# Cross-attention and a ternary-weight FFN on one core: weight group 0 with a scale of its own, partition-first inputs, a block order per phase, gate and up product signalled apart

## What is computed

```python
def xattn(h, ctx, Wq, Wk, Wv, Wo, gq, gk):        # 16 batches, 128 queries, 128 keys, 16 heads of 128
    q = rmsnorm((h @ Wq).reshape(B, Sq, H, D), gq)    # h: (16, 128, 256), Wq: (256, 2048)
    k = rmsnorm((ctx @ Wk).reshape(B, Skv, H, D), gk) # ctx: (16, 128, 128), Wk: (128, 2048)
    v = (ctx @ Wv).reshape(B, Skv, H, D)
    attn = softmax(einsum('bqhd,bkhd->bhqk', q, k) / sqrt(D))
    return einsum('bhqk,bkhd->bqhd', attn, v).reshape(B, Sq, H * D) @ Wo
def ffn(x, w_gate, w_up, w_down, ln_weight):      # bit_linear: x rounded to 8 bits per row, w to -1, 0, 1
    h = silu(bit_linear(x, w_gate)) * bit_linear(x, w_up)     # 256 -> 1024
    return bit_linear(rms_norm(h, ln_weight), w_down)         # 1024 -> 256
x = x + xattn(layernorm(x), ctx, ...)
x = x + ffn(layernorm(x), ...)
```

## Time and profile before

| | us |
|---|---|
| median of 3 runs | 482.82 |
| the three runs | 482.82, 481.75, 487.97 |
| the profiled execution, its own time | 481.36 |
| its span in the trace | 479.6 |

### The profile page before, as it was taken

The page is one execution under the profiler, slowest core; times in us unless marked ns, Lnnn a source line. Parts: engine busy times, 40 slices in busy tenths (PEclk is TensorE's granted clock), DMA queues, the critical chain, the costliest instruction groups (busy, mean ns, idle before and its releaser), DMA issues.

```text
span 479.6 us, 14503 instructions
## 1 busy us (share of the span) xinstructions
PE 408.6 (85%) x4459; PEld 308.8 (64%) x4459; DVE 431.3 (90%) x1237; ACT 434.9 (91%) x1459; POOL 393.2 (82%) x362
## 2 busy tenths in 40 slices
PE   0228776899999999999999999999999678789985
PEld 0127555687777877878777777777787455455564
DVE  0787899899999999999999999999998857999995
ACT  2298899999999999999999999999999579999983
POOL 1007568799999999999999999999998956878882
PEclk9986998899999999999999999999999899999999
DMA  7980464356554544545545455455564441011001
GB/s 261 355 258 12 128 192 88 66 112 130 111 114 88 121 98 96 122 88 110 109 88 122 97 103 115 88 111 110 97 116 100 93 84 25 0 34 33 22 33 57
DMA packets 145326, 50.18 MB, mean 105 GB/s; under 512 B 135952, under 2 KB 143120, under 8 KB 144784
## 3 DMA queue, kind: packets, MB, share of 16 engines
q1 hardware_dynamic: 144192, 46.68, 43.9%
q10 hardware_dynamic: 1104, 3.15, 1.9%
HBM read 14.16 MB, written 2.10 MB: 34 GB/s over the span
## 4 chain that ended last, share of the span: by engine, by line
ACT 50%; issue 16%; POOL 12%; DVE 8%; PE 8%; DMA 4%; ACTq 0%; POOLq 0%; SPq 0%; DVEq 0%
ACT work L655 15%; ACT kjunk L685 8%; ACT qhl L588 6%; ACT qshl L671 5%; POOL rkq L533 4%; DMA stage<-in_wq 3%; ACT work L673 3%; ACT ohl L692 3%; POOL work L525 2%; POOL phl L541 2%; PE KQ L375 2%; PE SO L375 2%; ACT stage L647 1%; POOL stage L554 1%; POOL qshl L516 1%
## 5 line engine op out<-in xcount | busy, mean ns | idle before, releaser
L375 PE MATMUL KQ<-hT,wqs 128*128 (+1 forms) x1536 | 102.7, 225 | 20.8 <-DVE qhl L912 16.2
L655 ACT ACTIVATE work<-SO,nbias,rkq 128x128 f32<-128x128 f32 x256 | 115.6, 483 | 3.1 <-DVE nbias L930 2.8
L533 POOL TENSOR_TENSOR rkq<-kqe,negh 128x8 f32<-128x8 f32 x65 | 111.8, 1721 | 5.0 <-DVE kqe L920 3.9
L375 PEld LDWEIGHTS KQ<-hT,wqs 128*128 128x128 f16 x1536 | 94.9, 101 | 28.1 <-issue 17.6
L516 POOL TENSOR_TENSOR qshl<-work,qshl 128x512 f16<-128x512 f32 x64 | 74.3, 1161 | 31.5 <-ACT work L673 31.4
L375 PE MATMUL EB<-As,ohl 128*128 128x256 f16 x768 | 96.4, 276 | 0.0
L375 PEld LDWEIGHTS EB<-As,ohl 128*128 128x128 f16 x768 | 76.2, 99 | 23.4 <-issue 0.8
L541 POOL TENSOR_TENSOR phl<-work,phl 128x512 f16<-128x512 f32 x64 | 74.1, 1158 | 7.2 <-DVE phl L970 5.4
L525 POOL TENSOR_TENSOR work<-work,rinv 128x512 f32<-128x512 f32 x64 | 66.6, 1041 | 4.3 <-DVE rinv L890 4.2
L375 PEld LDWEIGHTS SO<-kT,qhl 128*128 128x128 f16 x768 | 44.1, 98 | 31.4 <-DMA kT<-khl 20.3
L375 PE MATMUL SO<-kT,qhl 128*128 128x128 f16 x768 | 53.7, 219 | 7.1 <-ACT work L655 3.4
(11 more groups left out here) (153 smaller groups left out, 911.6 us busy)
## 6 DMA issues: line engine op xcount, KB each, us to landing
xs<-in_x SPq DMA_DIRECT2D x4, 512.0 KB, 8.8
wvo<-in_wo SPq DMA_DIRECT2D x1, 2048.0 KB, 24.6
out<-wqs SPq DMA_DIRECT2D x16, 128.0 KB, 1.7
raw<-in_ctxT ACTq DMA_DIRECT2D x1, 1024.0 KB, 5.8
stage<-in_wk SPq DMA_DIRECT2D x1, 1024.0 KB, 13.5
stage<-in_wq SPq DMA_DIRECT2D x1, 1024.0 KB, 16.5
stage<-in_wq ACTq DMA_DIRECT2D x1, 1024.0 KB, 12.8
kT<-khl SPq DMA_TRANSPOSE x64, 2.9
```

The lines of the kernel that those rows point to most:

```text
L375: last = matmul(out, lhsT=left(i), rhs=right(j), start=start and n == 0, stop=stop and n == 2)
L533: pool.tensor_tensor(rkq[:, g % 4, :], kqe[:, g % 2, :], negh[:, 0:2 * HG], ALU.pow).then_inc(root_ok, 1)
L655: ins = act.activation(pe[:, s, c], SB[:, c], ACT.Exp, scale=rkq[:, (g - AT_X + 1) % 4, HG + h:HG + h + 1], bias=nbias[:, s, h:h + 1], acc ...
```

## The change

The change has these parts.

1. **Inputs laid out partition first.** x, context, Wq (by group), Wv, Wo and the FFN weights are arranged on the host so that each partition's row is one contiguous piece (4 to 16 KB where 512 B to 4 KB were).
2. **Loads in SP's queue**, in the order x of batches 0 to 3, Wk of group 0, Wq of group 0, the rest of Wk, Wq of groups 1 to 3, Wv, Wo, context, the rest of x. ACT's queue keeps the transposed context and gq, gk.
3. **Group 0 has its own factors.** The first reduction takes the maximum over Wq group 0 and the sum over Wk group 0 only; a second reduction (`second_maxima` on PE, `maxima(2, ...)` on DVE) makes `scl[:, 4:6]` for groups 1 to 3. ACT's high splits of those wait for it.
4. **Squares of Wv and Wo** in ACT's queue at steps 0 (two) and 1 (one); the total and the factor of A (`TOT_AT`) at step 2, where it was step 1.
5. **An order per phase.** `step` is cut into named parts, called by `fill` (steps 0 to 3), `early` (4 to 7), `step` (the loop) and `drain` (after it).
6. **Gate and up split.** The gate product waits for the silu of the block before and signals silu by itself (`f_g`); the up product waits for h of the block before; silu writes two buffers in turn.

```diff
-SQ_AT = {0: (0, 1), 1: (1, 3)}
-STAT_AT = {0: (1, 3), 3: (3, 4)}
+SQ_AT = {0: (0, 2), 1: (2, 3)}
+STAT_AT = {0: (1, 3), 1: (3, 4)}
...
-        HI_AT = {'start': (0, 5), 0: (5, 9), 3: (9, 10), 4: (10, 11), 5: (11, 12)}
+        HI_AT = {'start': (0, 3), 0: (3, 8), 2: (8, 11), 3: (11, 12)}
...
             x_load(0)
-            sp.dma_start(wk_f, wk).then_inc(wk_in, 16)
-            sp.dma_start(wq_f[:, 1, :], wq[P:2 * P]).then_inc(wq_in[1], 16)
+            sp.dma_start(wk_f[:, 0:GW], wk[:, 0:GW]).then_inc(wk_in[0], 16)
+            sp.dma_start(wq_f[:, 0, :, :], wqP[:, 0, :, :]).then_inc(wq_in[0], 16)
+            sp.dma_start(wk_f[:, GW:INNER], wk[:, GW:INNER]).then_inc(wk_in[1], 16)
+            for g in range(1, G):
+                sp.dma_start(wq_f[:, g, :, :], wqP[:, g, :, :]).then_inc(wq_in[g], 16)
...
+            def second_maxima(b, g):
+                if now(b, g) == 0:
+                    te.wait_ge(amax2_ok, 1)
+                    te.wait_ge(asum_ok, 3)
+                    te.transpose(MB[0:2, P:2 * P], amax2[:, :], ident_f[:, :]).then_inc(gT_ps, 1)
+                    te.wait_ge(gdiag_ok, 2)
+                    te.matmul(MB[:, 8:10], lhsT=ones_f[0:2, :], rhs=gdiag[0:2, 0:2], start=True,
+                              stop=True).then_inc(gmax_ps, 1)
...
+                    need(te, f_sil, b, g, AT_GU, 1)
+                    ffn_product(KQ, wgq, s).then_inc(f_g, 1)
+                if live(b, g, AT_GU, B):
+                    s = (g - AT_GU) % 2
+                    need(te, f_xT, b, g, AT_GU)
                     need(te, f_hh, b, g, AT_GU, 1)
...
+                    ffn_product(TM, wuq, s).then_inc(f_gu, 1)
```

More of the change, by code:

```diff
@@ L323, in straight, with steps @@
                 step(s // G, s % G)
-        def steps(eng, step, ffn):
-            straight(step, 0, 2 * G)
+        def steps(eng, fill, early, step, drain, ffn):
+            straight(fill, 0, G)
+            straight(early, G, 2 * G)
             with eng.Fori(2, 2 + F_CHUNKS) as b:
@@ L542, in step, with fill, early, drain @@
                                        ALU.subtract).then_inc(plo_ok, 1)
+            def fill(b, g):
+                A_root(b, g)
+                roots_at(b, g)
+                q_square_low(b, g)
+                kq_roots(b, g)
+                c_lows(b, g)
+            def early(b, g):
+                q_square_low(b, g)
+                c_lows(b, g)
+                p_scaled(b, g)
+                kq_roots(b, g)
+                roots_at(b, g)
+                A_root(b, g)
+                p_low(b, g)
+            def step(b, g):
+                q_square_low(b, g)
+                p_scaled(b, g)
+                kq_roots(b, g)
+                p_low(b, g)
+            def drain(b, g):
+                ffn_roots_first(b, g)
+                q_square_low(b, g)
+                p_scaled(b, g)
+                kq_roots(b, g)
+                p_low(b, g)
             def ffn(b, g):
@@ L574, in ffn @@
                                        ALU.mult).then_inc(f_cg, 1)
-            steps(pool, step, ffn)
+            steps(pool, fill, early, step, drain, ffn)
         @block.scalar
@@ L736, in ffn @@
                     act.wait_ge(f_nm, 2)
-            steps(act, step, ffn)
+            steps(act, fill, early, step, drain, ffn)
         @block.vector
@@ L1172, in step, with fill, early, drain @@
                     ins.then_inc(e_ps, 1)
+            def fill(b, g):
+                scores(b, g)
+                second_maxima(b, g)
+                q_product(b, g)
+                k_product(b, g)
+                q_sums(b, g)
+                A_total(b, g)
+                A_products(b, g)
+                ln_transposed(b, g)
+            def early(b, g):
+                q_product(b, g)
+                k_product(b, g)
+                q_sums(b, g)
+                scores(b, g)
+                e_product(b, g)
+                A_products(b, g)
+                output(b, g)
+                A_total(b, g)
+                ln_transposed(b, g)
+                second_maxima(b, g)
+                ffn_sums(b, g)
+            def step(b, g):
+                q_product(b, g)
+                q_sums(b, g)
+                k_product(b, g)
+                scores(b, g)
+                output(b, g)
+                e_product(b, g)
+            def drain(b, g):
+                q_product(b, g)
+                q_sums(b, g)
+                k_product(b, g)
+                scores(b, g)
+                output(b, g)
+                e_product(b, g)
+            def ffn_product(banks, w, s):
+                for i in range(2):
+                    for k in range(KT):
+                        ins = te.matmul(banks[:, i * 512:(i + 1) * 512], lhsT=fxT[:, s, k, :],
+                                        rhs=w[:, k, i * 512:(i + 1) * 512], start=k == 0, stop=k == KT - 1)
+                return ins
             def ffn(b, g):
@@ L1219, in ffn @@
                     ins.then_inc(f_y, 1)
-            steps(te, step, ffn)
+            steps(te, fill, early, step, drain, ffn)
 _OUT = (B, SQ, DM)
```

339 lines of the change are left out of this document (259 added, 80 removed).

## The result

The changed kernel takes 480.42 us (median of 20 runs, 477.98 to 486.29), the kernel before 485.25 (20 runs beside them, 479.55 to 490.06). The ratio is 0.9924, 95% interval 0.9901 to 0.9947: 3.7 us faster (2.6 to 4.8), about half of the 7.0 that was forecast. The profiled execution took 482.9 us, its span is 481.1.

A forecast was written before the change was run, and what follows sets the result against it. ACT was taken to bound the start and, with other engines, a full loop; DVE's and ACT's work the FFN. Gains of 5.0 (start) and 2.0 (FFN) off 481.36 gave 474.4, 474.5 as median; range 470.5 to 480.0.

The forecast's parts named there:

- Nothing is to be had in it: Main loop: engines full and same instructions in the same order, so its length stays at 278.3 us.
- The first factors: Start, on DVE: ready at 13.8 instead of 23.08, 9.3 us earlier, needing only group 0 of Wk and Wq.
- near range: Start: the loads needed for the first factors land between 9.4, when gk is in, and 10.1.
- The ledger of ACT, 56.3 us and 1.0 idle: Steps 0 to 7: from q pieces at 28.4, ACT's work plus idle time puts the loop's start at 85.7.
- The start's gain, 5.0 us: Start and steps 0 to 7: the loop's first exponentials come at 85.7 against 90.71.
- The FFN, 2.0 us: FFN: splitting gate from up breaks a 4.5 us ring; blocks fall no lower than 4.4; bounds 0 and 3.85.
- The 0.5 for block 1: FFN: the part of its 2.0 us gained ahead, where block 1 waits for its silu.
- From the profile to the median: Whole kernel: 474.4 for a profiled execution became 474.5 for the changed kernel's median.
- early steps idle as before: Rival, steps 0 to 7: ACT's 4.26 us of waits stay and the FFN gives 1.0; 478.8 us, chance 0.16.
- The late first group: Rival, start: x of four batches lands at 11.18, Wk and Wq of group 0 at 13.1; 477.5 us, chance 0.09.
- the FFN weights ahead of the transposes: Rival, early steps: kT and pT wait behind 3 MB in SP's queue, delaying scores; 486.5 us, chance 0.05.
- the Trainium skill's rule on small transfers: Start: batch transfers to 1 MiB or more; by it the first loads land about 13.6, 3.5 us more.

The follow-up runs named there:

- before_freed: Kernel before with khl, kT, phl and pT at multiples of 512 bytes and kT's transpose ahead of pT's at every step; 479.23 us, ratio 0.986.
- loads_only: Kernel before with only the changed kernel's transfers, layouts and queues; block orders, factors and FFN as before; 483.77 us, ratio 0.995.
- gk_first: Changed kernel with gq and gk issued ahead of the transposed context on ACT's queue; 484.26 us, ratio 0.995.
- small_tiles_last: Changed kernel with its two new small tiles allocated behind all others, so khl, kT, phl and pT keep their old addresses; 478.00 us, ratio 0.986.
- aligned_512: Changed kernel with two unused tiles that put khl, kT, phl and pT each at a multiple of 512 bytes; 476.77 us, ratio 0.985.
- before_again: Kernel before, nothing edited, profiled a second time; 485.23 us.
- khl_off_64: Kernel before with unused tiles that move only khl, the transposes' source, 64 bytes beyond a multiple of 256; 487.83 us.

## Why the prediction was wrong

The forecast was 474.5; it was 480.4. Without the 2.9 us of the first point it would have been 477.5. By its own steps:

- **"Nothing is to be had in it", the loop of unchanged length.** The step that failed. "The same instructions in the same order" was true, and I took the same length from it. The transposes of k in it, whose order and bytes were the same, landed in 3.1 us for 2.9, and with p's transpose ahead of them in the queue that wait was on the path of the scores. Twelve iterations of 20.38 for 20.14 are 2.9 us lost, by two small tiles that moved khl by 64 bytes. Shown in both directions, and on the one side of the transposes. In the other direction the kernel had 6.7 us to gain by the same transposes (before_freed).
- **The first factors.** 14.88 for 13.8. The near range, 9.4 to 10.1 for the landings, had the right rows, but gk, which landed after 7.7 us in the earlier trace rows, took 9.4, with the same context ahead of it on ACT's queue and other transfers on SP's, and the maximum started at 11.34. In loads_only it took 10.7. It was one of three things due there: in gk_first the next, Wq's group 0, let it start at 10.7 and no earlier, and ACT's sums came last. Over six traces the q pieces come 4.1 us earlier (29.21 for 33.31 over seven), not 4.7.
- **The ledger of ACT, 56.3 us and 1.0 idle.** The work was right. The idle time was 2.56 us: 0.71 where I had 0.6, and 1.85 in step 3, where ACT waits for two products of Wv and Wo. PE did them near half its clock, in 1.93 and 1.91 us, where the pair of the step before took 1.11 and 1.03. Windows of PE (busy, clock, DMA share, GB/s), the changed kernel:

```profile
44.00:50.00 6.00, 5.07 (x54) 1.00 0.00 0
50.00:54.00 4.00, 1.47 (x16) 0.99 0.47 82
54.00:58.00 4.00, 4.00 (x19) 0.59 0.98 387
```

and small_tiles_last:

```profile
44.00:50.00 6.00, 5.91 (x21) 0.50 0.01 3
50.00:54.00 4.00, 4.00 (x50) 0.83 0.60 139
54.00:58.00 4.00, 3.92 (x42) 1.00 1.01 424
```

  In the first PE was idle for 2.5 of 4 us, and the granted clock then fell to 1.2 GHz just for the products that ACT wanted. In the second the low stretch came earlier, under a pair of products that ACT did not need yet: ACT waited 0.59 and reached the loop at 86.05, as near to the forecast (85.0 for this row) as any run came. I had priced every product of PE at the one clock that it had in its row.
- **The start's gain, 5.0 us.** 4.3 over seven and six traces (entries 91.3 and 87.0). The profile alone says 2.4, since it was made on an early entry of before. The forecast for this row was 85.0 from 89.99: the changed kernel came 2.0 later, by the two points above, and the kernel before comes 1.3 later than in the profile that I had, which hides most of it. The term is off by 0.7, and that it is so near is in part luck.
- **The FFN, 2.0 us.** 1.4, with a period of 4.42 in the row above, where I had 4.4 as the least. The 0.5 for block 1 came (its silu 4.01 behind the first, at 403.38 for 399.37; before 4.51), of the 1.5 behind it 0.9.
- **From the profile to the median.** I added 0.1 us to a profiled execution of 481.36, although the median of the three runs was 1.5 above it. Twenty runs have a median of 485.25, 3.9 above. The difference that I forecast, 7.0 us, stands beside 5.7 by the traces (4.3 and 1.4) without the iterations' loss, and 6.9 (4.4 to 9.4) by the ratio of small_tiles_last; the absolute time was forecast from a short execution.

The sum by what was measured: 4.3 and 1.4 gained, 2.9 lost, 2.8 us; the second profiles of both kernels lie 2.6 apart by their spans, and the ratio says 3.7 (2.6 to 4.8).

Of the rivals, "early steps idle as before" came no nearer than the forecast: 2.56 us idle lie about halfway between its 4.26 and the 1.0, and two thirds of them came of the clock, which neither had. Its price, 478.8, is the nearest to 480.4 of those on record, but by luck: the loss was in the loop. The late first group and the FFN weights ahead of the transposes did not come: the weights went out at 52.16, and the scores of step 5 came at 66.45 without waiting for a transpose behind them. Nor was the Trainium skill's rule on small transfers, cited in the prediction, borne out here: with x, Wk and Wq in pieces of 0.26 to 0.79 MB among them, all transfers together moved 357 GB/s over the first 29.30 us, where 313 were moved over the first 33.14 before.

What stays open: runs of one kernel spread over 8 to 10 us. The entry varies by 1.5 us over six traces of the changed start (86.05 to 87.57), and of the 1.5 between the two shown above 1.3 are ACT's waits, which go with the place of the clock's low stretch; over seven of the old one it varies by 2.8, and the first iteration by 2. The steps behind the last rounding took 84.0 and 84.6 us in the kernel before and 85.6 and 86.0 in the changed one, but 85.7 in small_tiles_last too, so this part of the loss is not shown to be the placement's. The rest was not traced. How the orders and the tables share their part wasn't separated.

## What to carry to other kernels

An edit that adds a tile moves every tile behind it: before saying that untouched code keeps its time, compare the addresses that transposes read from; put small tiles last. When two transfers share a queue, issue the one that is ready first, first; it does as much as making it faster. Take a start or a forecast from more than one profile: here the first was 3.9 us shorter than the median, as much as the effect.

## What was not expected of the hardware

How long a transpose by DMA occupies the DMA engines depends on where its source begins in a partition. Their packets are of nearly 256 bytes, and the time of one is worked out here from the queue's row: its share times 16 engines times 161 us, by the number of packets (stretch from 180 to 341 us; the share alone misleads a little, as the stretches hold 16.4 to 16.8 MB):

| kernel | khl, phl beyond a multiple of 256 | share of the DMA engines | packets | ns of one | kT lands | pT lands |
|---|---|---|---|---|---|---|
| aligned_512 | 0, 0 | 46.7% | 67653 | 17.8 | 2.8 | 2.8 |
| before_again | 0, 160 | 51.1% | 67460 | 19.5 | 2.9 | 3.2 |
| khl_off_64 | 64, 160 | 53.8% | 66063 | 21.0 | 3.1 | 3.2 |
| changed kernel | 64, 224 | 54.7% | 66827 | 21.1 | 3.1 | 3.2 |

The Trainium skill, "DMA: Bandwidth & Descriptors", section "How a descriptor splits into AXI transactions", has a rule that fits in direction: a read that doesn't begin at a multiple of 256 bytes begins at the multiple below, and what it fetches in vain counts. By it a 256-byte row that begins 64 beyond takes 10 beats of 32 bytes for 8, one that begins 160 beyond 13, one at 224 15; the sums for the four lines above are 16, 21, 23 and 25, an estimate from that page. The measured times rise in that order, but not in proportion: 1.7 ns for the first five beats, 1.5 for the next two, 0.1 for the last two. A source off its multiple costs, and how far off it is matters less here than the rule says: p lands in 3.2 us from 160 beyond and from 224 beyond. So these runs show that the source's place counts for a transpose, and not that fetched beats are the reason; places other than 0, 64, 160 and 224 beyond were not tried.

Two transfers of 4 bytes to each partition took 6.9 and 9.4 us to land behind 1 MB on their queue, and 4.7 and 6.2 at its head, at the price of 1.5 us for the start. Behind the same 1 MB on the same queue they took 6.1 and 7.7 us in the kernel before and 9.0 and 10.7 in loads_only, so what SP's queue carries beside it counts as well.
